# Gated slot attention: state matmuls ahead of the softmax transposes, and f and gate projections without a transpose

## The chip, the cores and the metric

The kernel runs on the 8 cores of one Trainium2 chip. Each core works on its own share of the batch, two sequences, with no exchange between cores. The metric is the device time of the slowest core in microseconds (us). Engines are TensorE (PE in the profile, its weight loads PEld), VectorE (DVE), ScalarE (ACT), GpSimd (POOL) and SyncE (SP). Each runs its own stream of instructions in order and waits for the others on semaphores.

## What is computed

One transformer layer on x of 16 x 2048 x 1024, float32. It has two halves with a residual each: gated slot attention, and a mixture of experts with top-1 routing. Cut to what matters, with H = 8 heads, DK = 128 and M = 64 slots:

```python
q, k, v = silu(x @ Wq), silu(x @ Wk), x @ Wv
log_f   = log_sigmoid(x @ Wf1 @ Wf2);  s = 1 - exp(log_f)
# per head, over time:
hk = hk * exp(log_f)[:, None] + k[:, None] * s[None, :];  ok = q @ hk
qv = softmax(ok)
hv = hv * exp(log_f)[:, None] + s[:, None] * v[None, :];  ov = qv @ hv
out = ov * sigmoid(x @ Wg1 @ Wg2);  out = rmsnorm_per_head(out) * norm_w
x = x + out @ Wo          # x on the right is the layer norm of the input
x = x + p_max * gelu(ln(x) @ W1[e]) @ W2[e]     # e = argmax of the router, 8 experts
```

## The kernel before

**Tiling.** A core does its two sequences b = 0, 1 one after the other: attention of b, then the FFN of b. The sequence lies in x_buf in SBUF. Attention goes through it in 16 segments of 128 positions, each of two chunks of 64. The recurrence is worked out per chunk, with the states a_hk and a_hv carried between them. The FFN then runs every expert over groups of 1024 positions. Its weights are converted to bf16 in DRAM by DMAs that start at the beginning.

**Order of the work.** The order is written out by hand: `P.op` (its issuing line is line 60 for all instructions of the profile) appends an instruction to the stream of an engine, `P.wait` a wait on a semaphore. On VectorE and ScalarE every operation waits for the one before it and increments a semaphore of its engine.

**Input groups.** `make_x_groups(s)` gives 17 groups for segment s: g1 (layer norm), g2 (transposes), six projections (q, k, v in halves, called q0, q1, k0, k1, v0, v1 here), g6 (the f gate: x @ Wf1, then @ Wf2), g6b and two g6c (the output gate), g7 (sigmoids), g8a and g8b (transposes of q and k), g9 and g9b (decay factors, with the triI and triL matmuls). Each group writes the one PSUM bank p_x; ScalarE evacuates it, and the next group waits for that (`px_wait`). The groups of segment 0 run ahead of the loop, as a prologue. For the others g1 goes ahead of `emit_y` of the segment before, and the rest are fed in by `inject()`, two groups at a call, of which `emit_y(s)` has two per chunk and two after both; g8a to g9b follow it. In the last segment of a sequence nothing is left to feed in.

**In g6 and g6b** the eight matmuls of x @ Wf1 (or Wg1) have the activations xnt as stationary operand and give a 128 x 128 result with positions as rows. It is evacuated (a_u, a_ug), transposed by TensorE, evacuated again (a_ut, a_ugt), and only then multiplied by Wf2 (Wg2).

**A chunk in `emit_y`**, in the order of TensorE's stream: the ones128 matmul into p_st (waiting for the state update and the output step before it), the 16 onescol matmuls into p_st with a small exp behind them (blast_act), 8 matmuls k.q into p_a, 16 into p_ok, `inject()`; VectorE and ScalarE work out the softmax of p_ok; 16 transposes into p_tp, 8 matmuls into p_a, 16 into p_ov; then 24 state matmuls: per head one of k and s into p_st and two of s and v into p_st2 (heads 0 to 3) or p_ok (heads 4 to 7); `inject()`. VectorE's state update (a_hk from p_st, then a_hv from p_st2 and p_ok, 8 operations) waits for the last of the 24. After both chunks: gate, norm, transposes into p_tp, 16 matmuls with Wo into p_ov, and the addition to x_buf.

Of the kernel before, what the change touches and what calls it, by code (L numbers as in the profile page):

```python
# [8 lines left out]
AF = mybir.ActivationFunctionType  # L9
# [70 lines left out]
def build_nc():  # L80
# [228 lines left out]
    def emit_attention(b):  # L309
# [17 lines left out]
        def px_wait():  # L327
            if "free" in px_state:
                P.wait(t, px_state["free"][0], px_state["free"][1])

        def make_x_groups(s):
# [49 lines left out]
            def g6():  # L381
                def small_mm_t(dst_sb, w1sb):
                    px_wait()
                    for dt in range(8):
                        p1 = P.op(t, "matmul", p_x[:, 0:DK],
                                  S["xnt"][:, dt * SEG:(dt + 1) * SEG],
                                  w1sb[:, dt * DK:(dt + 1) * DK],
                                  start=(dt == 0), stop=(dt == 7),
                                  inc="pe" if dt == 7 else None)
                    P.wait(a, "pe", p1)  # L390
                    e1 = P.op(a, "activation", dst_sb, p_x[:, 0:DK], AF.Copy,
                              inc="act")
                    evac_done("act")
                    return e1

                def tr(dst_sb, src_sb, e1):
                    px_wait()
                    p1 = P.op(t, "transpose", p_x_b[:, 0:DK], src_sb, id128[:],
                              inc="pe")
                    P.wait(a, "pe", p1)  # L400
                    e2 = P.op(a, "activation", dst_sb, p_x_b[:, 0:DK], AF.Copy,
                              inc="act")
                    evac_done("act")
                    return e2

                e1 = small_mm_t(a_u[:], a_wf1)
                e2 = tr(a_ut[:], a_u[:], e1)
# [8 lines left out]
            def g6b():  # L416
                def small_mm_t(dst_sb, w1sb):
                    px_wait()
                    for dt in range(8):
                        p1 = P.op(t, "matmul", p_x[:, 0:DK],  # L420
                                  S["xnt"][:, dt * SEG:(dt + 1) * SEG],
                                  w1sb[:, dt * DK:(dt + 1) * DK],
                                  start=(dt == 0), stop=(dt == 7),
                                  inc="pe" if dt == 7 else None)
# [584 lines left out]
```

How the kernel before makes its waits and increments, by code:

```python
        def f(e, fname=fname, args=args, kw=kw, h=h, amt=amt):  # L59
            ins = getattr(e, fname)(*args, **kw)
            if h is not None:
                ins.then_inc(h, amt)
# [8 lines left out]
        def f(e, h=h, val=val):  # L71
            e.wait_ge(h, val)
```

## Time and profile before

| | us |
|---|---|
| median of 2 timed runs | 12,627.6 |
| lowest, highest | 12,280.6, 12,974.7 |
| the profiled execution | 11,624.9 |
| its span, slowest core (core 3) | 11,623.4 |
| spans of the eight cores | 11,592.4 to 11,623.4 |
| mean granted TensorE clock of the cores | 0.843 to 0.845 |

The profile is of one execution, on its slowest core. The granted clock is a share of full speed: 1.00 is 2.4 GHz, 0.50 is 1.2 GHz. In a row of the timeline stand the start, the duration, the engine, the operation with what it writes and reads, how many instructions are merged, and in brackets how long the engine had been idle and what released it. The state matmuls show as p_st (64*128 64x64), and as p_st and p_ok (64*64 64x128); p_st2 is listed as p_st, and rows of the two forms are partly merged. Merged rows overlap a little, as the ends of matmuls are modelled.

### The profile page before, as it was taken

The numbers are of one execution on the slowest core, as the hardware profiler recorded it, in microseconds if no ns is written. First come the engines' busy times: TensorE is split into PE (matmuls) and PEld (weight loads), VectorE is DVE, ScalarE is ACT, GpSimd is POOL, SyncE is SP. The second block draws the span as 40 slices with busy tenths as digits, with TensorE's granted clock in tenths as the row PEclk, the third lists the DMA queues.
The fourth block names the chain that finished last, engine by engine and source line by source line (L and its number), as shares of the span: only waits on it lengthen the run. The fifth ranks groups of instructions, "written<-read, shape, count | busy, mean of one in ns | idle before, by whom it ended". The sixth has DMA issues, their size and how long they took to land.

```text
span 11623.4 us, 114796 instructions; the slowest of 8 cores (11592.4 to 11623.4 us)
## 1 busy us (share of the span) xinstructions
PE 9248.6 (80%) x44448; PEld 4228.6 (36%) x44448; DVE 1755.1 (15%) x2899; ACT 2237.4 (19%) x3340; POOL 1377.4 (12%) x2414
## 2 busy tenths in 40 slices
PE   2555555999999999999935555559999999999999
PEld 1222222444444444444412222224444444444443
DVE  2333333000000000000023333330000000000000
ACT  1212222211121112211112122222112211122111
POOL 0000000111111111111100000001111111111111
PEclk7555556999999999999955555579999999999999
DMA  9999501333333433333330000013333334333333
GB/s 139 110 110 109 58 1 33 93 110 111 104 98 104 124 116 96 105 102 109 108 73 1 1 1 1 1 33 100 108 115 98 102 104 122 112 98 102 107 109 114
DMA packets 262991, 999.45 MB, mean 86 GB/s; under 512 B 44832, under 2 KB 45088, under 8 KB 258352
## 3 DMA queue, kind: packets, MB, share of 16 engines
q0 software_dynamic: 254176, 958.56, 34.7%
q1 hardware_dynamic: 8288, 33.55, 0.8%
q8 instruction: 369, 6.05, 0.2%
q14 instruction: 158, 1.29, 0.0%
HBM read 1128.14 MB, written 150.99 MB: 110 GB/s over the span
## 4 chain that ended last, share of the span: by engine, by line
PE 76%; DVE 11%; ACT 6%; issue 4%; another core or an unknown queue 2%; DMA 1%; DVEq 0%; ACTq 0%; POOL 0%; POOLq 0%
PE p_ov L60 26%; PE p_st L60 24%; PE p_x L60 9%; DVE arena L60 8%; PE p_ok L60 6%; ACT arena L60 5%; PE p_tp L60 5%; PE p_a L60 4%; DVE x_buf L60 3%; ACT L60 1%; DMA arena<-w2sc 1%; DVEq L72 0%; ACTq L72 0%; DMA arena<-wr 0%
## 5 line engine op out<-in xcount | busy, mean ns | idle before, releaser
L60 PE MATMUL p_ov<-arena 128*128 128x512 bf16 (+1 forms) x13824 | 3484.9, 389 | 338.5 <-DVE x_buf L60 170.9
L60 PE MATMUL p_st<-arena 128*128 128x512 bf16 (+2 forms) x13312 | 3267.7, 373 | 20.4 <-DVE x_buf L60 20.4
L60 PEld LDWEIGHTS p_ov<-arena 128*128 128x128 bf16 (+1 forms) x13824 | 1392.2, 106 | 2008.6 <-issue 634.5
L60 PEld LDWEIGHTS p_st<-arena 128*128 128x128 bf16 (+2 forms) x13312 | 1291.3, 99 | 1578.7 <-issue 80.8
L60 PE MATMUL p_x<-arena 128*128 128x512 bf16 (+2 forms) x4448 | 1511.7, 427 | 221.7 <-ACT arena L60 213.1
L60 ACT ACTIVATE arena<-p_ov,arena 128x512 bf16<-128x512 f32 x1024 | 703.6, 687 | 4672.2 <-PE p_ov L60 4624.5
L60 POOL DMA_DIRECT2D arena<-w2sc x2048 | 1099.5, 537 | 3474.6 <-PE p_tp L60 3473.0
L60 DVE SCALAR_TENSOR_TENSOR x_buf<-p_ov,arena,x_buf 128x512 f32<-128x512 f32 x128 | 96.1, 750 | 7028.1 <-PE p_tp L60 7021.1
L60 PE MATMUL p_ok<-arena 128*128 128x512 bf16 (+3 forms) x3584 | 1062.5, 337 | 73.7 <-DVE arena L60 64.7
L60 PE MATMUL p_a<-arena 128*128 128x512 bf16 (+2 forms) x3072 | 862.5, 333 | 90.5 <-DVE arena L60 81.5
L60 ACT ACTIVATE arena<-p_st,arena 128x512 bf16<-128x512 f32 x1024 | 703.7, 687 | 1040.6 <-PE p_st L60 991.2
L60 PE MATMUL p_tp<-arena 128*128 128x512 bf16 x2048 | 785.7, 384 | 8.6 <-DVE x_buf L60 8.6
L60 PEld LDWEIGHTS p_x<-arena 128*128 128x128 bf16 x4448 | 448.1, 113 | 883.4 <-issue 605.9
L60 ACT ACTIVATE arena<-p_x 128x512 bf16<-128x512 f32 (+3 forms) x512 | 305.9, 597 | 2098.7 <-PE p_x L60 2093.0
L60 POOL DMA_DIRECT2D arena<-w1sc x256 | 226.9, 888 | 3124.7 <-PE p_st L60 2695.8
L60 PE MATMUL p_tp<-id,arena 64*64 64x64 bf16 (+2 forms) x1600 | 130.0, 253 | 562.2 <-DVE arena L60 544.1
L60 PE MATMUL p_x<-id,arena 128*128 128x128 bf16 x832 | 109.8, 294 | 528.4 <-DVE arena L60 369.0
L60 PEld LDWEIGHTS p_ok<-arena 128*128 128x128 bf16 (+2 forms) x3584 | 362.4, 110 | 414.0 <-issue 104.5
L60 DVE TENSOR_TENSOR arena<-arena 64x512 f32<-64x512 f32 (+5 forms) x484 | 349.1, 721 | 940.0 <-ACT arena L60 542.8
L60 POOL DMA_DIRECT2D arena<-b x4 | 2.1, 523 | 3582.3 <-DVE x_buf L60 3582.3
L60 PEld LDWEIGHTS p_a<-arena 128*128 128x128 bf16 (+2 forms) x3072 | 261.1, 113 | 357.2 <-issue 122.8
L60 PEld LDWEIGHTS p_tp<-id,arena 64*64 64x64 bf16 (+2 forms) x1600 | 108.0, 142 | 631.8 <-issue 631.8
(84 smaller groups left out, 2536.5 us busy)
## 6 DMA issues: line engine op xcount, KB each, us to landing
arena<-w2sc POOLq DMA_DIRECT2D x2048, 256.0 KB, 2.9
arena<-w1sc POOLq DMA_DIRECT2D x256, 1024.0 KB, 6.1
w1sc<-w POOLq DMA_DIRECT2D x8, 8192.0 KB, 418.2
w2sc<-w POOLq DMA_DIRECT2D x8, 8192.0 KB, 1027.0
x_buf<-x SPq DMA_DIRECT2D x2, 8192.0 KB, 44.7
y<-x_buf SPq DMA_DIRECT2D x4, 4096.0 KB, 12.2
arena<-wq POOLq DMA_DIRECT2D x2, 2048.0 KB, 30.5
arena<-wk POOLq DMA_DIRECT2D x2, 2048.0 KB, 45.9
```

What stands on the lines that cost most here:

```text
L60: ins = getattr(e, fname)(*args, **kw)
```

## The change

In g6 and g6b the operands of the eight matmuls are swapped, so that the result comes out transposed, and the transpose and one evacuation are dropped. In each chunk, the eight p_st state matmuls are issued behind the first `inject()`, and the sixteen p_st2 and p_ok ones behind them with a wait for the VectorE product that reads p_ok; both groups stand ahead of the wait for the softmax. The state update waits for the last p_ov matmul. The number of state matmuls and their operands are the same.

```diff
--- before.py
+++ after.py
@@ -379,32 +379,17 @@
                 return f
 
             def g6():
-                def small_mm_t(dst_sb, w1sb):
-                    px_wait()
-                    for dt in range(8):
-                        p1 = P.op(t, "matmul", p_x[:, 0:DK],
-                                  S["xnt"][:, dt * SEG:(dt + 1) * SEG],
-                                  w1sb[:, dt * DK:(dt + 1) * DK],
-                                  start=(dt == 0), stop=(dt == 7),
-                                  inc="pe" if dt == 7 else None)
-                    P.wait(a, "pe", p1)
-                    e1 = P.op(a, "activation", dst_sb, p_x[:, 0:DK], AF.Copy,
-                              inc="act")
-                    evac_done("act")
-                    return e1
-
-                def tr(dst_sb, src_sb, e1):
-                    px_wait()
-                    p1 = P.op(t, "transpose", p_x_b[:, 0:DK], src_sb, id128[:],
-                              inc="pe")
-                    P.wait(a, "pe", p1)
-                    e2 = P.op(a, "activation", dst_sb, p_x_b[:, 0:DK], AF.Copy,
-                              inc="act")
-                    evac_done("act")
-                    return e2
-
-                e1 = small_mm_t(a_u[:], a_wf1)
-                e2 = tr(a_ut[:], a_u[:], e1)
+                px_wait()
+                for dt in range(8):
+                    p1 = P.op(t, "matmul", p_x[:, 0:SEG],
+                              a_wf1[:, dt * DK:(dt + 1) * DK],
+                              S["xnt"][:, dt * SEG:(dt + 1) * SEG],
+                              start=(dt == 0), stop=(dt == 7),
+                              inc="pe" if dt == 7 else None)
+                P.wait(a, "pe", p1)
+                e2 = P.op(a, "activation", a_ut[:], p_x[:, 0:SEG], AF.Copy,
+                          inc="act")
+                evac_done("act")
                 px_wait()
                 P.wait(t, "act", e2)
                 p1 = P.op(t, "matmul", p_x[:], a_ut[:], a_wf2[:], start=True,
@@ -414,25 +399,15 @@
                 evac_done("act")
 
             def g6b():
-                def small_mm_t(dst_sb, w1sb):
-                    px_wait()
-                    for dt in range(8):
-                        p1 = P.op(t, "matmul", p_x[:, 0:DK],
-                                  S["xnt"][:, dt * SEG:(dt + 1) * SEG],
-                                  w1sb[:, dt * DK:(dt + 1) * DK],
-                                  start=(dt == 0), stop=(dt == 7),
-                                  inc="pe" if dt == 7 else None)
-                    P.wait(a, "pe", p1)
-                    e1 = P.op(a, "activation", dst_sb, p_x[:, 0:DK], AF.Copy,
-                              inc="act")
-                    evac_done("act")
-                    return e1
-                e3 = small_mm_t(a_ug[:], a_wg1)
                 px_wait()
-                p1 = P.op(t, "transpose", p_x_b[:, 0:DK], a_ug[:], id128[:],
-                          inc="pe")
+                for dt in range(8):
+                    p1 = P.op(t, "matmul", p_x[:, 0:SEG],
+                              a_wg1[:, dt * DK:(dt + 1) * DK],
+                              S["xnt"][:, dt * SEG:(dt + 1) * SEG],
+                              start=(dt == 0), stop=(dt == 7),
+                              inc="pe" if dt == 7 else None)
                 P.wait(a, "pe", p1)
-                xs["ugt"] = P.op(a, "activation", a_ugt[:], p_x_b[:, 0:DK], AF.Copy,
+                xs["ugt"] = P.op(a, "activation", a_ugt[:], p_x[:, 0:SEG], AF.Copy,
                                  inc="act")
                 evac_done("act")
 
@@ -582,12 +557,20 @@
                                tile_position=(0, pi * 64),
                                inc="pe" if h == 7 else None)
                 inject()
+                P.wait(t, "act", ys["blast_act"])
+                for h in range(H):
+                    P.op(t, "matmul", p_st[:, h * 64:h * 64 + 64],
+                         S["ktm"][rs, h * 128:(h + 1) * 128],
+                         S["stb"][rs, h * 64:(h + 1) * 64],
+                         start=True, stop=True, tile_position=(pi * 64, 0),
+                         inc="pe" if h == 7 else None)
                 P.wait(v, "pe", pok)
                 okb = a_otmp[rs, 0:512]
                 qvt = a_otmp[rs, 512:1024]
                 okb3 = okb.rearrange("p (h m) -> p h m", m=64)
                 qvt3 = qvt.rearrange("p (h m) -> p h m", m=64)
-                P.op(v, "tensor_tensor", okb, p_ok[rs, :], S["B"][rs, :], ALU.mult)
+                okb_dve = P.op(v, "tensor_tensor", okb, p_ok[rs, :], S["B"][rs, :],
+                               ALU.mult, inc="dve")
                 P.op(v, "tensor_reduce", a_nmx[rs, :], okb3, axis=AX.X, op=ALU.max,
                      negate=True)
                 sm_dve = P.op(v, "tensor_tensor", qvt3, okb3,
@@ -602,6 +585,18 @@
                      a_rsum[rs, :].unsqueeze(2).broadcast_to([64, 8, 64]), ALU.mult)
                 qb_dve = P.op(v, "tensor_tensor", a_qb[rs, :], qvt, S["B"][rs, :],
                               ALU.mult, inc="dve")
+                P.wait(t, "dve", okb_dve)
+                for h in range(H):
+                    sbc = S["stb"][rs, h * 64:(h + 1) * 64]
+                    vv = S["vtm"][rs, h * 128:(h + 1) * 128]
+                    bank2 = p_st2 if h < 4 else p_ok
+                    for base in (0, 64):
+                        pov_st = P.op(t, "matmul",
+                                      bank2[base:base + 64,
+                                            (h % 4) * 128:(h % 4 + 1) * 128],
+                                      sbc, vv, start=True, stop=True,
+                                      tile_position=(pi * 64, base),
+                                      inc="pe" if (h == 7 and base == 64) else None)
                 P.wait(t, "dve", qb_dve)
                 for h in range(H):
                     oc = h * 64
@@ -635,25 +630,14 @@
                     P.op(t, "matmul", p_ov[rs, h * 128:(h + 1) * 128],
                          a_atm[rs, h * 64:h * 64 + 64], vv,
                          start=True, stop=False, tile_position=(pi * 64, pi * 64))
-                    P.op(t, "matmul", p_ov[rs, h * 128:(h + 1) * 128],
-                         a_qbt[rs, oc:oc + 64], a_hv[rs, h * 128:(h + 1) * 128],
-                         start=False, stop=True, tile_position=(pi * 64, pi * 64))
-                for h in range(H):
-                    sbc = S["stb"][rs, h * 64:(h + 1) * 64]
-                    vv = S["vtm"][rs, h * 128:(h + 1) * 128]
-                    P.op(t, "matmul", p_st[:, h * 64:h * 64 + 64],
-                         S["ktm"][rs, h * 128:(h + 1) * 128],
-                         sbc, start=True, stop=True, tile_position=(pi * 64, 0))
-                    bank2 = p_st2 if h < 4 else p_ok
-                    for base in (0, 64):
-                        pov = P.op(t, "matmul",
-                                   bank2[base:base + 64,
-                                         (h % 4) * 128:(h % 4 + 1) * 128],
-                                   sbc, vv, start=True, stop=True,
-                                   tile_position=(pi * 64, base),
-                                   inc="pe" if (h == 7 and base == 64) else None)
+                    ov_pe = P.op(t, "matmul", p_ov[rs, h * 128:(h + 1) * 128],
+                                 a_qbt[rs, oc:oc + 64],
+                                 a_hv[rs, h * 128:(h + 1) * 128],
+                                 start=False, stop=True,
+                                 tile_position=(pi * 64, pi * 64),
+                                 inc="pe" if h == 7 else None)
                 inject()
-                P.wait(v, "pe", pov)
+                P.wait(v, "pe", ov_pe)
                 P.wait(v, "act", bca_act)
                 P.op(v, "tensor_tensor", a_hkt, a_hk, a_bca, ALU.mult)
                 P.op(v, "tensor_tensor", a_hk, a_hkt, p_st[:], ALU.add)
```

## Rows read from the trace of the kernel before

**Rows 1.** The page: busy TensorE and its granted clock in 40 slices, tenths.
```profile
PE   2555555999999999999935555559999999999999
...
PEclk7555556999999999999955555579999999999999
```

**Rows 2.** Busy time by stretch: PE, PEld, DVE, ACT, POOL, then granted clock, DMA.
```profile
100.00:1860.00 1760.00, 897.12 (x5352) 461.88 (x5352) 615.75 (x1104) 370.41 (x586) 3.73 (x5) 0.59 0.70 77
...
2300.00:5800.00 3500.00, 3364.37 (x15120) 1486.99 (x15118) 174.06 (x232) 619.79 (x902) 619.36 (x1082) 0.97 0.36 107
```

**Rows 3.** Timeline, first chunk: start, duration, engine, operation, idle before and its releaser.
```profile
1018.83 3.08 PE L60 MATMUL p_ok<-arena 64*64 64x64 bf16 x16 [1.01 <-DVE arena L60]
...
1022.08 0.68 DVE L60 TENSOR_TENSOR arena<-p_ok,arena 64x512 f32<-64x512 f32 x1 [3.40 <-PE p_ok L60]
...
1024.19 3.40 PE L60 MATMUL p_x<-arena 128*128 128x512 bf16 x8 [1.32 <-ACT arena L60]
...
1028.44 0.63 ACT L60 ACTIVATE arena<-arena 64x512 f32<-64x512 f32 x1
...
1031.93 1.03 PE L60 MATMUL p_tp<-id,arena 64*64 64x64 bf16 x16 [4.34 <-DVE arena L60]
...
1035.94 1.88 PE L60 MATMUL p_ov<-arena 64*64 64x128 bf16 x16 [1.12 <-DVE arena L60]
...
1037.75 1.86 PE L60 MATMUL p_st<-arena 64*128 64x64 bf16 x13
...
1041.02 3.54 PE L60 MATMUL p_x<-arena 128*128 128x512 bf16 x8
...
1041.34 0.43 DVE L60 TENSOR_TENSOR arena<-arena 128x512 bf16<-128x512 bf16 x1 [5.66 <-PE p_ok L60]
...
1044.46 1.70 DVE L60 SCALAR_TENSOR_TENSOR arena<-arena,p_ok 128x128 bf16<-128x128 bf16 x4
...
1045.45 1.89 PE L60 MATMUL p_x<-arena 128*128 128x512 bf16 x8 [0.89 <-ACT arena L60]
...
1047.27 0.39 PE L60 MATMUL p_st<-arena,ones 64*128 64x512 bf16 x1
```

**Rows 4.** Timeline, second chunk and the head of what follows it.
```profile
1064.41 0.74 PE L60 MATMUL p_tp<-id,arena 64*64 64x64 bf16 x16 [4.36 <-DVE arena L60]
...
1070.13 1.87 PE L60 MATMUL p_st<-arena 64*128 64x64 bf16 x13
...
1073.72 0.43 DVE L60 TENSOR_TENSOR arena<-arena 128x512 bf16<-128x512 bf16 x1 [5.82 <-PE p_ok L60]
...
1086.98 1.01 PE L60 MATMUL p_tp<-id,arena 128*128 128x128 bf16 x8 [1.32 <-DVE arena L60]
```

**Rows 5.** Timeline of TensorE in the prologue of the first batch.
```profile
135.50 0.22 PE L60 MATMUL p_x<-id,arena 128*128 128x128 bf16 x1 [0.57 <-ACT arena L60]
...
136.40 0.58 PE L60 MATMUL p_x<-arena 128*128 128x512 bf16 x1 [0.68 <-ACT arena L60]
```

**Rows 6.** Timeline: triI matmul of g9 for segments 1, 2, 3 and 15 (of 0 to 15).
```profile
263.86 0.64 PE L60 MATMUL p_x<-arena,triI 64*64 64x512 bf16 x2 [4.42 <-DVE arena L60]
...
367.26 0.64 PE L60 MATMUL p_x<-arena,triI 64*64 64x512 bf16 x2 [4.42 <-DVE arena L60]
...
475.76 0.64 PE L60 MATMUL p_x<-arena,triI 64*64 64x512 bf16 x2 [4.43 <-DVE arena L60]
...
1742.99 0.64 PE L60 MATMUL p_x<-arena,triI 64*64 64x512 bf16 x2 [4.43 <-DVE arena L60]
```

**Rows 7.** Granted clock around q1 of rows 3; a slow q1 and k0, second segment.
```profile
1038.00:1041.00 3.00, 3.00 (x23) 1.65 (x23) 0.00 (x0) 0.00 (x0) 0.00 (x0) 0.50 1.18 131
...
1044.00:1045.00 1.00, 0.56 (x2) 0.00 (x0) 0.78 (x3) 0.29 (x1) 0.00 (x0) 0.81 0.31 33
...
403.88 3.60 PE L60 MATMUL p_x<-arena 128*128 128x512 bf16 x8
...
408.37 3.57 PE L60 MATMUL p_x<-arena 128*128 128x512 bf16 x8 [0.89 <-ACT arena L60]
```

## The prediction

> **What bounds the kernel now.** I read the strip of forty slices first, then the busy times by stage, then the timeline of one segment, then the starts of all segments.
>
> The strip shows four stages: two stretches in which TensorE is about half busy at about half of its full clock (slices 2 to 7 and 22 to 27), each followed by a long stretch at 9 and near full clock [rows 1]. The busy times by stage put numbers on it. In the first attention stretch (100 to 1860 us) TensorE works 897 of 1760 us, VectorE 616 and ScalarE 370, at a mean granted clock of 0.59; the second looks the same in the strip. In the FFN stretch TensorE works 3364 of 3500 us at 0.97 [rows 2]. So the FFN is bound by TensorE, and attention by no engine: it is a chain of short steps in which the engines wait for each other. The diff touches only attention. Whatever it saves there starts the FFN earlier by the same time; the FFN itself should not change.
>
> The timeline of one segment shows where the chain runs. A segment has two chunks. In the first one TensorE ends projection q0 at 1027.59 (1024.19 + 3.40), and then sits idle for 4.34 us until the softmax chain on ScalarE (exp at 1028.44, queued behind the evacuation of q0) and VectorE frees the 16 transposes at 1031.93. Then come p_ov at 1035.94 and, right behind it, the 24 state matmuls, from 1037.75 to the start of the next projection q1 at 1041.02. VectorE starts the state update only after them, at 1041.34 [rows 3]. The second chunk repeats it: idle until the transposes at 1064.41, state matmuls at 1070.13, state update at 1073.72 [rows 4].
>
> **The change, part by part.**
>
> 1. *The 24 state matmuls move* from behind p_ov to a place between the first pair of injected projections and the softmax transposes. What they leave: from 1037.75 to 1041.02 they take 3.27 us of TensorE. In the first chunk q1 stood right behind them, and behind q1 come its evacuation, k0 (1045.45) and, at 1047.27, the matmul that opens the next chunk. That matmul also waits for the state update. The update's last group starts at 1044.46 and takes 1.70, so it ends at 1046.16, 1.1 us before the opener [rows 3]. Both branches start 3.27 us earlier, so the opener does too. In the second chunk VectorE's chain (state update at 1073.72, then gate, norm and scale up to the transposes at 1086.98, 13.26 us later) sets the end. It begins 3.59 us after the state matmuls begin (1070.13), just as in the first chunk (1037.75 to 1041.34) [rows 3, 4]. With the wait on p_ov alone it begins 3.27 us earlier. So 2 x 3.27 = 6.54 us leave each segment.
>
> 2. *Where they go.* The eight p_st matmuls need only the small exp, long done; the other sixteen need the VectorE product that reads p_ok, which starts at 1022.08 and takes 0.68, done 4.8 us before q0 ends [rows 3]. So all 24 can start at 1027.59 without a wait. The place has 4.34 us. The price is at most what they cost in the old order, 3.27 us or 0.136 each, and at least 2.8 us if all went at the p_ov price (1.88 / 16 = 0.117 each). Even the interleaved p_ok group (3.08 / 16 = 0.193 each, the dearest narrow row) would make 4.6 us, 0.3 over the gap [rows 3]. In the new order the two forms stand in separate groups, so I take something at or below 3.27 and nothing on the path. If the p_ok price held, it would cost 0.3 x 64 = 19 us. ScalarE has both projection evacuations and exp in its queue ahead of anything the moved matmuls could delay. The new wait for the VectorE product has only the sixteen matmuls and the transposes behind it, and is released earlier.
>
>    In the last segment of a batch nothing is injected. There the moved matmuls meet the wait for the p_ok product, but have the whole softmax chain as cover, from 1022.08 to 1031.93 less the evacuation of q0. All 2 x 16 segments save the same: 32 x 6.54 = 209 us.
>
> 3. *f and gate projections without the transposes.* The eight matmuls swap operands and yield the transposed result directly; a transpose, its wait and its evacuation leave. In the prologue this is on the chain: from the transpose at 135.50 to the next matmul at 136.40 is 0.90 us [rows 5]. Two such places in each of two batches give 3.6 us. Within segments the same work lies beside VectorE's 13.26 us chain of the second chunk [rows 4]: nothing. If that cover were gone, it would be worth 0.9 x 2 x 30 = 54 us more.
>
> 4. *Waits.* The VectorE product's added semaphore costs nothing, since every VectorE operation increments one already.
>
> Sum: 209 + 3.6 = 213 us. The profiled execution took 11,624.9 us (span 11,623.4), so its own time would become 11,412. The two timed runs of the kernel lie at 12,280.6 and 12,974.7, median 12,627.6: well above the profiled one, and 694 us apart. Carried over to the median: 12,627.6 - 213 = 12,415.
>
> **The clock.** The level that TensorE is granted moves the segment time. The first interval between segments is 103.40 us, the second 108.50, and the mean of the fourteen between 263.86 and 1742.99 is 105.65 [rows 6]. The difference is the projections: k0 takes 1.89 us at the upper level (2.4 GHz) and 3.57 at the lower (1.2 GHz) [rows 3, 7]. What raises the level? While p_ov and the state matmuls kept TensorE fully busy the granted clock stayed at 0.50; it rose only when q1, which starts at 1041.02, was ending (0.81 over 1044 to 1045) [rows 7]. No rise followed directly on the stretch that is taken away, and q1 and k0 themselves stay as they are. So I take the mix of fast and slow segments to stay too.
>
> Against that stands a rule. The Trainium skill, in "TensorE: Matmul & The Clock Gate", section "Why this matters for your kernels", advises keeping TensorE continuously busy to get past its throttled state. By the rule, taking 3.27 us of unbroken work away ahead of q1 would lose fast groups. The rows just named speak against it, and another pair does: q1 and k0 of the second segment stood behind the same unbroken state matmuls, and k0 was slow all the same [rows 7].
>
> **The rivals.**
>
> - *Clock lost.* If every segment after were like the slowest (108.50 instead of 105.65), the loss is 2.85 x 30 = 86 us, and 127 us remain: 12,501. For it: the removed unbroken stretch. Against it: the rows above. 10%.
> - *Clock gained.* If every one were like the fastest (103.40), 2.25 x 30 = 68 us more, 281 us in all: 12,347. For it: a shorter segment packs its projections closer. Against: nothing makes the projections themselves denser. 14%.
> - *Half of it.* One chunk's saving is taken by another wait, for instance because in the first chunk the update proves late and the opener waits for VectorE. The margin is 1.1 us here, and both sides move together. 105 + 3.6 = 109 us: 12,519. 6%.
> - *Slower.* The FFN runs at another granted clock. It is the only stage large enough: two FFN stretches, the first with 3364 of 3500 us of TensorE work [rows 2] and the second alike in the strip. A granted clock lower by 3% in both costs 0.03 x 2 x 3364 = 202 us and eats the saving; to end over 2% slower it takes 213 + 253 = 466 us, a clock lower by 7%. For it: the 694 us between two runs of one kernel, which no latency-bound stage could give. Against: nothing in the change touches the FFN. A draw of that kind may fall either way. I give it 30%: 20% that it makes the result more than 2% faster, 4% within, 6% slower.
> - The forecast as it stands: 40%.
>
> **How the numbers follow.** Two per cent of 12,628 is 253 us, about what a measurement of this kernel can tell from no change. The forecast (213, 1.7%) lies inside, clock lost and half inside too, clock gained outside. Faster: 14 + 20 = 34%; within: 40 + 10 + 6 + 4 = 60%; slower: 6%. The likeliest case alone, with runs like the median, saves 194 (the p_ok price) to 213 us, 12,415 to 12,434. The full range must hold the spread of the runs: from the profiled execution less 213, 11,410, to the slower run less 213, 12,760.
>
> **What would show it.** Right: the 24 matmuls stand at the end of q0, end before the transposes, and the idle time ahead of the transposes shrinks from 4.34 us to 1.1 us or a little more, the transposes not later; VectorE's update starts 0.2 to 0.3 us after p_ov ends; segment starts are 99 us apart on average instead of 105.65; the FFN stretches are as long as before. Wrong: transposes later than 4.34 us behind q0 (cover too small), a mean segment above 101 us with k0 and v0 mostly at 3.57 us (clock), the opener waiting for VectorE (half).

## The result and the profile after

| | kernel before | changed kernel |
|---|---|---|
| median of the timed runs, us | 12,338.6 (10 runs) | 12,152.3 (11 runs) |
| lowest run, us | 11,623.2 | 11,398.1 |
| profiled execution, us | 11,624.9 | 11,398.3 |
| first attention stretch, us | 1715.7 | 1600.1 |
| second attention stretch, us | 1710.9 | 1603.0 |
| first FFN stretch to the next batch, us | 4089.8 | 4089.0 |

The changed kernel is faster: the ratio of like runs is 0.9807, with a 95% interval from 0.9779 to 0.9836. Whether the gain is more or less than 2% this leaves open. An attention stretch is counted from TensorE's first instruction of a batch to the 32 small transposes that open the FFN (113.67 to 1829.41 and 5919.16 to 7630.10 before, 104.59 to 1704.71 and 5793.72 to 7396.71 after). The runs of one kernel differ by several hundred us, because in many of them the cores of a die get a lower clock in the FFN; so attention stretches are compared below.

The strip of the page after, busy TensorE and its granted clock in tenths, keeps the shape of [rows 1], with attention stretches that end earlier:

```profile
PE   3445546999999999999834545469999999999998
...
PEclk7565558999999999999955565589999999999999
```

Busy time by stretch after (columns as in [rows 2]). Attention is still far from full on any engine, at a granted clock of 0.60 (0.59 before), and the FFN still has 0.97:

```profile
100.00:1700.00 1600.00, 788.88 (x5187) 425.60 (x5264) 588.50 (x1069) 356.81 (x545) 0.55 (x2) 0.60 0.76 83
...
2300.00:5500.00 3200.00, 3054.80 (x13570) 1361.26 (x13845) 162.12 (x216) 594.96 (x866) 551.02 (x956) 0.97 0.37 106
```

The timeline of two chunks after answers to [rows 3, 4]. The trace has lost one matmul record of some projection groups, which is why they read "x7" and seem to start 0.4 us late. (p_st2 is again listed as p_st.)

```profile
1050.11 0.68 DVE L60 TENSOR_TENSOR arena<-p_ok,arena 64x512 f32<-64x512 f32 x1 [3.40 <-PE p_ok L60]
...
1052.60 3.19 PE L60 MATMUL p_x<-arena 128*128 128x512 bf16 x7 [1.70 <-DVE arena L60]
...
1055.72 1.17 PE L60 MATMUL p_st<-arena 64*128 64x64 bf16 x16
...
1056.68 0.64 PE L60 MATMUL p_ok<-arena 64*64 64x128 bf16 x8
...
1060.13 1.03 PE L60 MATMUL p_tp<-id,arena 64*64 64x64 bf16 x16 [2.81 <-DVE arena L60]
...
1064.14 1.88 PE L60 MATMUL p_ov<-arena 64*64 64x128 bf16 x16 [1.12 <-DVE arena L60]
...
1066.27 0.42 DVE L60 TENSOR_TENSOR arena<-arena 128x512 bf16<-128x512 bf16 x1 [2.39 <-PE p_ov L60]
...
1066.36 3.19 PE L60 MATMUL p_x<-arena 128*128 128x512 bf16 x7 [0.33 <-issue]
...
1069.39 1.70 DVE L60 SCALAR_TENSOR_TENSOR arena<-arena,p_ok 128x128 bf16<-128x128 bf16 x4
...
1070.44 3.57 PE L60 MATMUL p_x<-arena 128*128 128x512 bf16 x8 [0.89 <-ACT arena L60]
...
1073.95 0.60 PE L60 MATMUL p_st<-arena,ones 64*128 64x512 bf16 x1
...
1088.30 0.74 PE L60 MATMUL p_st<-arena 64*128 64x64 bf16 x16
...
1088.88 0.39 PE L60 MATMUL p_ok<-arena 64*64 64x128 bf16 x8
...
1092.72 1.03 PE L60 MATMUL p_tp<-id,arena 64*64 64x64 bf16 x16 [3.45 <-DVE arena L60]
...
1098.89 0.42 DVE L60 TENSOR_TENSOR arena<-arena 128x512 bf16<-128x512 bf16 x1 [2.38 <-PE p_ov L60]
```

The 16 matmuls of p_st and p_st2 stand at the end of q0 (1055.72), the 8 of p_ok behind them. All 24 are through at 1057.32, after 1.60 us at the lower clock; in the second chunk, at the upper one, from 1088.30 they take 0.97 us. TensorE then still waits 2.81 us for the softmax. p_ov ends at 1066.02, and VectorE's update starts 0.25 us later, at 1066.27. It ends at 1071.09, 2.9 us ahead of the opener of the next chunk at 1073.95. So TensorE's q1 and k0 set the end of the first chunk, as they did before (the margin was 1.1 us there; k0 is slow here and was fast there).

The 226.6 us between the two profiled executions add up so. TensorE's first instruction comes 9.1 us earlier (104.59 in place of 113.67); over the eight cores of all these kernels it lies anywhere from 102 to 116 us, so that is no effect of the change. Attention gives 115.6 and 107.9 us. The first FFN stretch is 0.7 us shorter, and the rest of the run, from the second FFN start to the end, is 6.7 us longer. These are two single cores. In means over the eight cores an attention stretch takes 1712.6 us before and 1598.5 after, 114.1 less.

### The profile page after: what moved, and what is told of

Same layout as the page of the kernel before. It is cut to its first block, busy times and chain, and to the rows that moved or that the text cites. A ratio compares the mean times of both kernels' runs of the same rounds, so it can differ in the third digit from the quotient of the medians.

```text
span 11396.7 us, 113717 instructions; the slowest of 8 cores (11362.1 to 11396.7 us)
## 1 busy us (share of the span) xinstructions
PE 8997.2 (79%) x43561; PEld 4163.8 (37%) x44384; DVE 1755.5 (15%) x2899; ACT 2219.0 (19%) x3276; POOL 1377.2 (12%) x2414
## 4 chain that ended last, share of the span: by engine, by line
PE 74%; DVE 12%; ACT 6%; issue 4%; another core or an unknown queue 2%; DMA 1%; DVEq 1%; ACTq 0%; POOL 0%; POOLq 0%
PE p_ov L60 27%; PE p_st L60 23%; DVE arena L60 9%; PE p_x L60 9%; PE p_ok L60 6%; ACT arena L60 5%; PE p_tp L60 5%; PE p_a L60 4%; DVE x_buf L60 3%; ACT L60 1%; DMA arena<-w2sc 1%; DVEq L72 1%; ACTq L72 0%; DMA arena<-wr 0%
## 5 line engine op out<-in xcount | busy, mean ns | idle before, releaser
L60 PE MATMUL p_ov<-arena 128*128 128x512 bf16 (+1 forms) x13556 | 3438.4, 388 | 361.3 <-DVE x_buf L60 179.6
L60 PE MATMUL p_st<-arena 128*128 128x512 bf16 (+2 forms) x13054 | 3132.7, 370 | 40.5 <-DVE x_buf L60 23.6
L60 PEld LDWEIGHTS p_st<-arena 128*128 128x128 bf16 (+1 forms) x13312 | 1248.5, 99 | 1546.8 <-issue 114.8
L60 PE MATMUL p_x<-arena 128*128 128x512 bf16 (+2 forms) x4221 | 1423.8, 423 | 306.2 <-ACT arena L60 216.5
L60 PE MATMUL p_ok<-arena 128*128 128x512 bf16 (+3 forms) x3584 | 1012.8, 328 | 77.4 <-DVE arena L60 64.7
L60 PE MATMUL p_a<-arena 128*128 128x512 bf16 (+2 forms) x3002 | 837.3, 333 | 90.5 <-DVE arena L60 81.5
L60 ACT ACTIVATE arena<-p_x 128x512 bf16<-128x512 f32 (+1 forms) x448 | 287.9, 643 | 1888.4 <-PE p_x L60 1599.6
```

Source lines behind the costliest of these rows:

```text
L60: ins = getattr(e, fname)(*args, **kw)
```

## The experiments

The table has one core of each kernel, for the doubled kernel ("moved, twice") two. Over the eight cores of a profile a first or second stretch varies by 2 to 18 us in most kernels. It varies by 50 and 36 us in the doubled kernel, and by 40 us in the first stretch of the last one. "Fast" counts the projection groups (eight 128x512 matmuls) that took 1.89 us, of 192; the prologues hold up to ten of them.

| kernel | core | attention stretches, us | mean segment interval in each, us | fast |
|---|---|---|---|---|
| before | 3 | 1715.7, 1710.9 | 105.8, 105.8 | 42 |
| changed | 0 | 1600.1, 1603.0 | 98.8, 99.0 | 41 |
| only moved | 4 | 1601.9, 1602.5 | 99.0, 98.9 | 43 |
| only projections | 3 | 1709.8, 1712.4 | 105.8, 105.8 | 38 |
| only regrouped, old place | 0 | 1656.9, 1655.7 | 102.4, 102.4 | |
| moved, not regrouped | 4 | 1595.2, 1602.6 | 98.6, 99.0 | |
| moved, twice | 0 | 1655.1, 1643.7 | 102.2, 101.5 | 24 |
| the same profile | 3 | 1606.5, 1615.2 | 99.0, 99.8 | 65 |
| first chunk only | 0 | 1645.2, 1654.3 | 101.6, 102.2 | |
| second chunk only | 0 | 1659.5, 1655.9 | 102.5, 102.4 | |
| changed, 1 copy more | 0 | 1601.0, 1607.2 | 99.0, 99.2 | 66 |
| changed, 3 copies more | 4 | 1655.4, 1654.9 | 102.4, 102.5 | 40 |
| changed, fillers | 4 | 1597.9, 1593.3 | 98.9, 98.4 | 41 |
| changed, p_ok grouped | 4 | 1547.9, 1544.7 | 95.6, 95.4 | 39 |
| the same, again | 5 | 1545.3, 1542.2 | 95.6, 95.2 | |
| p_ok grouped and fillers | 4 | 1515.4, 1547.6 | 93.6, 95.6 | |

The count varies from core to core too: 37 to 43 in the kernel before, 40 to 47 in the changed one. Two of the three runs of the kernel "first chunk only" took 22,377 and 24,624 us, and one of nine of "the same, again" 25,992 us; why isn't on record.

**Which half of the diff gains.** First the move alone, with the projections of the kernel before:

```diff
-                for dt in range(8):
-                    p1 = P.op(t, "matmul", p_x[:, 0:SEG], a_wf1[...], S["xnt"][...], ...)
+                e1 = small_mm_t(a_u[:], a_wf1)
+                e2 = tr(a_ut[:], a_u[:], e1)
```

> The changed kernel with the f and gate projections of the kernel before (transposes kept), so only the state matmuls are moved. Theory (the moved matmuls carry the gain): about 223 us under the kernel before in like runs (11,400 to 11,405), mean segment interval 99.0 us, as in the changed kernel. Rival (the dropped transposes count within segments): at least 50 us less gain, 11,450 or more.

The stretches are 1601.9 and 1602.5 us, the changed kernel's to 2 us, and the mean interval is 99.0 us, as expected. Then the projections alone, in the kernel before:

```diff
-                e1 = small_mm_t(a_u[:], a_wf1)
-                e2 = tr(a_ut[:], a_u[:], e1)
+                for dt in range(8):
+                    p1 = P.op(t, "matmul", p_x[:, 0:SEG], a_wf1[...], S["xnt"][...], ...)
```

> The kernel before with only the f and gate projections changed (operands swapped, no transposes). Theory: covered by VectorE's chain within segments, 3.6 us in the prologues, about 11,621 in a like run, mean segment interval unchanged at 105.7 us. Rival (half hidden): 30 us or more less and an interval 1 us shorter.

1709.8 and 1712.4 us against 1715.7 and 1710.9. The interval stays at 105.8, and 30 us are excluded: the transposes in the groups were hidden. The effect forecast for the prologues, 1.8 us each, is lost in the spread of single stretches, but not in the prologues themselves. From TensorE's first instruction of a batch to the first triI matmul they take 43.6 us before and 42.0 with the projections alone, in means over eight cores and both batches (44.3 with the move alone, 41.8 in the changed kernel). The move is the gain.

**Each chunk by itself.** The move is made where `c4` is 0, or where it is 1; in the other chunk the 24 stay behind p_ov.

```diff
+                if c4 == 0:      # second kernel: c4 == 1
+                    P.wait(t, "dve", okb_dve)
+                    for h in range(H):
+                        ...
+                if c4 != 0:
+                    for h in range(H):
+                        ... as in the kernel before, behind p_ov
```

> State matmuls moved (grouped) in the first chunk of each segment only; the second chunk and the f and gate projections as in the kernel before. Theory (each chunk gives its own 3.27 us, here by way of TensorE's order): mean segment interval 105.8 - 3.3 = 102.5 us, attention stretch 1713 - 54 = 1659. Rival (only the second chunk's move pays, as there VectorE's chain is the longer): 105.8 and 1713.

> State matmuls moved in the second chunk only; the first chunk and the projections as in the kernel before. Theory: here VectorE's chain starts 3.27 us earlier, mean interval 102.5 us, stretch 1659. Rival (the first chunk carries it all): 105.8 and 1713.

Each gives about half: 1645 to 1654 us and 1656 to 1660 us. Both chunks lay on the way to the end, as forecast. That it was TensorE's order in the one and VectorE's chain in the other is read from the rows, and neither run separates them.

**Is it the place or the grouping?** The diff does two things to the state matmuls: it moves them, and it issues eight of one tile form and then sixteen of another in place of alternating per head. Grouping alone, in the old place:

```diff
                 for h in range(H):
-                    sbc = ...; vv = ...
-                    P.op(t, "matmul", p_st[:, h * 64:h * 64 + 64], ...)
+                    P.op(t, "matmul", p_st[:, h * 64:h * 64 + 64], ...)
+                for h in range(H):
+                    sbc = ...; vv = ...
                     bank2 = p_st2 if h < 4 else p_ok
                     for base in (0, 64):
```

> The kernel before with the 24 state matmuls left behind p_ov, but issued as eight p_st ones and then sixteen p_st2/p_ok ones instead of alternating per head. Theory 1 (alternating between tile forms is what cost 3.27 us; grouped the 24 take 1.60 us as in the changed kernel at the lower clock): 1.67 us less per chunk, 64 x 1.67 = 107 us, about 11,518, and VectorE's state update starts 1.9 us after p_ov ends. Theory 2 (they were short in the changed kernel because of their place, behind an idle stretch or at another clock): no gain, 11,625.

Timeline on core 5, behind p_ov (TensorE, then VectorE's update):

```profile
1028.15 1.88 PE L60 MATMUL p_ov<-arena 64*64 64x128 bf16 x16 [1.28 <-DVE arena L60]
...
1029.96 1.17 PE L60 MATMUL p_st<-arena 64*128 64x64 bf16 x16
...
1030.92 0.63 PE L60 MATMUL p_ok<-arena 64*64 64x128 bf16 x8
...
1031.49 3.19 PE L60 MATMUL p_x<-arena 128*128 128x512 bf16 x8
...
1031.81 0.42 DVE L60 TENSOR_TENSOR arena<-arena 128x512 bf16<-128x512 bf16 x1 [4.08 <-PE p_ok L60]
```

From 1029.96 to the next projection at 1031.49 the 24 take 1.53 us in place of 3.27, and the update starts 1.78 us after p_ov ends. The stretches fall by 59 and 55 us, to 1656.9 and 1655.7: half of the gain of the change is to be had without moving anything. So alternating was dear. Then the other way round, the new place with the old order:

```diff
-                for h in range(H):
-                    P.op(t, "matmul", p_st[...], ..., tile_position=(pi * 64, 0), ...)
-                P.wait(t, "dve", okb_dve)   # behind the softmax product's issue
+                P.wait(t, "dve", okb_dve)
+                for h in range(H):
+                    P.op(t, "matmul", p_st[...], ..., tile_position=(pi * 64, 0))
+                    ... the two of bank2
```

> The changed kernel with the state matmuls in the new place, but alternating per head as in the kernel before. Theory (the cover of 4.34 us holds either order): the 24 take 3.27 us, the idle time of TensorE ahead of the softmax transposes is 1.1 us in place of 2.8, and the time equals the changed kernel's within 10 us (11,400). Rival (the grouping matters for the time): about 100 us slower than the changed kernel, 11,500.

1595.2 and 1602.6 us: the changed kernel's time. Alternating is dear here too: TensorE's idle time ahead of the transposes is 1.45 us in first chunks and 1.91 in second ones, in means over eight cores, where the changed kernel has 3.10 and 3.46. But the order doesn't matter for the time, because the gap covers either. That the gap is a cover of limited size shows when the alternating 24 are issued twice each (extra work):

```diff
-                for h in range(H):
+                for h in [hh for hh in range(H) for _ in range(2)]:
```

> The changed kernel with the state matmuls alternating per head and each issued twice, in the new place: 48 matmuls, 6.54 us by the rows of the kernel before, in a gap of 4.34 us. Theory (the gap is a cover of that size): the softmax transposes come 2.2 us late in each chunk, mean segment interval 98.9 + 4.4 = 103.3 us, stretch about 1670. Rival (the gap is not what limits): 1600 us as before, or the whole 3.27 us a chunk on top, 1705.

Timeline, TensorE, second chunk of a segment on core 1:

```profile
1018.60 2.26 PE L60 MATMUL p_x<-arena 128*128 128x512 bf16 x8 [0.89 <-ACT arena L60]
...
1020.79 2.76 PE L60 MATMUL p_st<-arena 64*128 64x64 bf16 x25
...
1025.84 0.31 PE L60 MATMUL p_ok<-arena 64*64 64x128 bf16 x2
...
1025.96 1.05 PE L60 MATMUL p_tp<-id,arena 64*64 64x64 bf16 x16
```

v0 ends at 1020.86, the 48 fill the time to the transposes at 1025.96, and no idle time stands ahead of these. They come 5.1 us behind v0 in place of 4.36, here with part of the group at the upper clock. In means of the eight cores they come 5.4 to 6.2 us behind q0 and 5.0 to 5.2 behind v0 (4.4 in both places in the changed kernel), with no idle time ahead of them in any segment. So the gap is a cover of limited size, and what sticks out is 1.6 to 2.6 us a segment, where 4.4 was expected at the lower clock throughout.

What becomes of that differs within the same profile. On core 0 the stretches are 55 and 41 us longer than in the changed kernel. On core 3 they are 6 and 12 us longer, and the first stretches of cores 6 and 7 are 1605.2 and 1606.9 us, with the changed kernel's interval of 99.0. The rival of no effect nearly holds there, and the whole 6.5 us a segment is found nowhere. A segment of core 3 (q0, the transposes, k0, v0):

```profile
1062.47 3.23 PE L60 MATMUL p_x<-arena 128*128 128x512 bf16 x8 [1.32 <-ACT arena L60]
...
1070.99 1.06 PE L60 MATMUL p_tp<-id,arena 64*64 64x64 bf16 x16
...
1080.62 1.89 PE L60 MATMUL p_x<-arena 128*128 128x512 bf16 x8 [0.89 <-ACT arena L60]
...
1093.48 1.89 PE L60 MATMUL p_x<-arena 128*128 128x512 bf16 x8 [0.89 <-ACT arena L60]
```

There k0 was fast in all 30 segments and v0 in 27, on core 0 in 17 and 4. Faster groups took back most of what the late transposes cost. The next two experiments show the same.

**Why 6.9 us a segment where 6.54 were taken away.** A known delay is put on the path: the copy of a_qbt on VectorE is made once more, or three times more.

```diff
                 P.op(v, "tensor_copy", a_qbt[rs, :], p_tp[rs, 0:512])
+                P.op(v, "tensor_copy", a_qbt[rs, :], p_tp[rs, 0:512])
```

> The changed kernel with one redundant copy more on VectorE in each chunk, on the path between the softmax transposes and p_a (the copy of a_qbt made twice; a copy starts every 0.52 us). Adding up rows: 2 x 0.52 = 1.0 us a segment, mean interval 99.9, stretch 1617. If the mix of fast and slow projection groups shifts against it, as it may have done in the change (6.9 us gained where 6.54 were taken away): the interval stays at 98.9 to 99.2, stretch 1600 to 1604.

> The same with three redundant copies more in each chunk, 6 x 0.52 = 3.1 us a segment. Adding up rows: mean interval 102.0, stretch 1650. If the mix shifts: back to the 102.4 us that the kernel with regrouped matmuls in the old place had, stretch 1656, with fewer fast groups than the 41 of 187 of the changed kernel.

Starts of the triI matmul in the second batch, segments 0 and 15, in the kernel before, the changed one, and with one and three copies more:

```profile
5961.71 0.63 PE L60 MATMUL p_x<-arena,triI 64*64 64x512 bf16 x2 [4.43 <-DVE arena L60]
...
7549.29 0.64 PE L60 MATMUL p_x<-arena,triI 64*64 64x512 bf16 x2 [4.43 <-DVE arena L60]
```

```profile
5837.40 0.64 PE L60 MATMUL p_x<-arena,triI 64*64 64x512 bf16 x2 [4.43 <-DVE arena L60]
...
7321.92 0.64 PE L60 MATMUL p_x<-arena,triI 64*64 64x512 bf16 x2 [4.43 <-DVE arena L60]
```

```profile
5826.86 0.64 PE L60 MATMUL p_x<-arena,triI 64*64 64x512 bf16 x2 [4.43 <-DVE arena L60]
...
7315.14 0.64 PE L60 MATMUL p_x<-arena,triI 64*64 64x512 bf16 x2 [4.43 <-DVE arena L60]
```

```profile
5901.75 0.64 PE L60 MATMUL p_x<-arena,triI 64*64 64x512 bf16 x2 [4.43 <-DVE arena L60]
...
7438.50 0.63 PE L60 MATMUL p_x<-arena,triI 64*64 64x512 bf16 x2 [4.43 <-DVE arena L60]
```

A fifteenth of each difference is the mean interval: 105.84, 98.97, 99.22 and 102.45 us. One copy more adds 1.04 us of work to a segment and 0.25 us to the interval. Three add 3.12 us and the interval grows by 3.5. The mix of fast and slow groups answers. Within segments only k0 and v0, the second of their pairs, were ever at 1.89 us. Of their 60 groups 32 were fast in the kernel before, 58 with one copy more and 30 with three. In means, k0 and v0 took 2.84 and 2.49 us before, 2.90 and 2.34 in the only moved kernel, 1.95 and 1.95 with one copy more, 2.06 and 3.40 with three. Wo (the 16 matmuls into p_ov at the segment's end) goes the other way with one copy more, 6.3 us where the changed kernel has 5.5, and takes 5.6 with three.

The intervals found in the kernels without fillers lie near 105.8, 102.4, 98.9 and 95.5 us, each 3.4 to 3.5 us from the next, whatever was added or taken. The first-chunk kernel (101.6 in one of its stretches) and the doubled one (99.8 to 102.2 besides 99.0) come off these. In means over eight cores and both batches:

| change | taken from or added to a segment, us | interval, us |
|---|---|---|
| grouping in the old place | -3.5 | 105.82 to 102.35 |
| the move alone | -6.5 | 105.82 to 98.86 |
| the changed kernel | -6.5 | 105.82 to 98.75 |
| one copy more in it | +1.0 | 98.75 to 99.08 |
| three copies more in it | +3.1 | 98.75 to 102.42 |
| p_ok grouped in it (below) | -3.8 | 98.75 to 95.43 |

So a change moves the mean interval by about 0, one or two steps of 3.4 us, whichever is nearest. That the interval moves in steps is shown; why the steps are of this size no run shows.

**Can the clock be raised?** Idle time of TensorE is filled with full-width matmuls whose result nobody reads, in three gaps of each chunk.

```diff
+                for _ in range(5):
+                    P.op(t, "matmul", p_a[:], a_wq[:, 0:128], a_wq[:, 0:512],
+                         start=True, stop=True)
                 P.wait(t, "dve", qb_dve)
... (two into p_a ahead of tt_dve's wait, two into p_x ahead of atm2_dve's)
```

> The changed kernel with idle time of TensorE filled by full-width matmuls whose result nobody reads (extra work, the output is unaffected): five ahead of the softmax transposes, two between the transposes and p_a, two between p_a and p_ov, in each chunk. Theory (the clock level is what makes a segment long or short, and TensorE's wide work raises it): more of the projection groups take 1.89 us instead of 3.57 than the 41 of 187 of the changed kernel, and the attention stretch falls below 1600 us, by up to 90 (about 6 us a segment if all of them were fast, 1510). Rival (the gaps don't matter to the level, or the fillers run over the gaps): 1600 us or more.

Timeline, first chunk of a segment, slowest core (core 7):

```profile
1067.87 1.25 PE L60 MATMUL p_a<-arena 128*128 128x512 bf16 x5
...
1071.38 0.66 PE L60 MATMUL p_tp<-id,arena 64*64 64x64 bf16 x16 [2.26 <-DVE arena L60]
...
1071.97 0.60 PE L60 MATMUL p_a<-arena 128*128 128x512 bf16 x2
...
1073.71 1.03 PE L60 MATMUL p_x<-arena 128*128 128x512 bf16 x2
...
1074.89 1.88 PE L60 MATMUL p_ov<-arena 64*64 64x128 bf16 x16
...
1076.71 3.60 PE L60 MATMUL p_x<-arena 128*128 128x512 bf16 x8
```

The five fillers ahead of the transposes and the two behind them ran at the upper clock (0.25 to 0.30 us each). The last two (1.03 us) were back at the lower one, and the eight matmuls of q1, behind p_ov, still took 3.60 us. 41 of 192 groups were fast, as before (36 to 44 over the eight cores). Stretches of 1597.9 and 1593.3 us are 2 to 10 us better; in means over the cores it is 1 us. The theory failed in this form.

**The same cost elsewhere.** The 16 matmuls of p_ok alternate two forms as well (3.08 us in [rows 3]) and stand on the path. They are grouped; the start flag is set at head 0 alone.

```diff
+                for h in range(H):
+                    P.op(t, "matmul", p_ok[rs, oc], a_atm[rs, oc], S["stl"][...],
+                         start=(h == 0), stop=False, tile_position=(pi * 64, pi * 64))
                 for h in range(H):
-                    P.op(t, "matmul", p_ok[rs, oc], a_atm[rs, oc], ..., start=True, ...)
-                    pok = P.op(..., S["qt"][:, tc], a_hk[:, oc], start=False, stop=True, ...)
+                    pok = P.op(..., S["qt"][:, tc], a_hk[:, oc], start=False, stop=(h == 7), ...)
```

> The changed kernel with the 16 p_ok matmuls grouped as well: first the eight of 64 rows (a_atm), then the eight of 128 rows, instead of alternating per head. Theory (alternating forms is what is dear, and this group stands on the path in both chunks): the group takes 1.2 to 1.3 us (eight p_a matmuls of either form take 0.60 to 0.64) instead of 3.08, so about 1.85 us less per chunk, 64 x 1.85 = 118 us, an attention stretch of about 1541 us in place of 1600, about 11,280 in a run like the profiled one. Rival (the alternation costs nothing, K = 128 or the accumulation does): no gain.

Timeline, the p_ok group in both chunks of a segment and the transposes that follow the first:

```profile
1024.69 1.17 PE L60 MATMUL p_ok<-arena 64*64 64x64 bf16 x16 [1.00 <-DVE arena L60]
...
1025.79 1.03 PE L60 MATMUL p_x<-id,arena 128*128 128x128 bf16 x8
...
1053.21 1.03 PE L60 MATMUL p_ok<-arena 64*64 64x64 bf16 x16 [1.01 <-DVE arena L60]
```

1.17 us in place of 3.08, both at the lower clock, and stretches of 1547.9 and 1544.7 us, 52 and 58 less than in the changed kernel. The grouping also parts the two matmuls that add to the same sum. That this was dear is unlikely: the p_ov matmuls of [rows 3] add up in such pairs, in one form, and take 0.117 us each with twice the columns, where p_ok alternating took 0.193. It was run again:

> The kernel with the grouped p_ok matmuls once more, timed in more rounds beside the kernel before. Theory: the attention stretch is again 1540 to 1548 us, the mean interval 95.2 to 95.6, and the fastest run lies 112 + 227 = 339 us under the fastest of the kernel before, near 11,285. Rival (the shorter attention is paid back by a longer FFN): the first FFN stretch is longer than 4093 us and the fastest run no better than the changed kernel's 11,398.

The stretches repeat (1545.3 and 1542.2; 1542.8 and 1541.6 on core 7), and the first FFN stretch is 4087 us, no longer than before. Its fastest run took 11,299.3 us (11,285 was expected), beside 11,625.1 for the fastest of the kernel before: 326 us, 2.8%, and 99 us under the changed kernel's fastest. This kernel beats both. With the fillers added:

> The grouped p_ok matmuls and the fillers together (the fillers are extra work whose result nobody reads). If both theories hold and add: attention stretch about 1450 to 1540 us, 11,100 to 11,280. If the shorter p_ok group leaves less work ahead of q0 and the clock falls back: no better than the grouped one alone.

1515.4 and 1547.6 us, and a fastest run of 11,275.3 us, 24 us less. The first stretch is 32 us shorter and the second 3 us longer than with the grouping alone. The other cores agree: the first stretch is 1513 to 1531 us on six of eight (1546 to 1553 on cores 2 and 3), against 1545 to 1552 with the grouping alone, and the second one doesn't gain on any. So the fillers gained something in one place, with an interval of 93.3 to 94.6 us that no other kernel has; why not in the other stretch stays open. Of a single pair of fastest runs 24 us would prove nothing.

## Why the prediction was right and wrong

**The mechanism was right.** Moved matmuls leave the path and are covered, in both chunks, VectorE's update starts 0.25 us after p_ov, the FFN is untouched. In attention the two stretches gave 223.6 us on the cores read, and 228 in means over the eight cores, against 213 forecast.

**The term that was mis-sized is 6.54 us a segment.** It was 6.9 on the cores read (105.84 to 98.97), and 7.07 in means over eight cores and both batches (105.82 to 98.75). The 228 us add up so: 30 intervals of 7.07 make 212 where 196 were forecast, the two last segments about 6.3 each (6.54 forecast), and the two prologues 1.7 each (1.8). So the intervals alone are off. The step that failed is "So I take the mix of fast and slow segments to stay too": the interval does not follow the sum of what is on the path, it moves in steps of about 3.4 us, and 6.54 us taken away became two of them. How the two came to differ is found in the durations in part. In these means v0 takes 2.50 us before and 2.34 after, Wo 5.63 and 5.47, k0 2.83 and 2.85: 0.3 of the 0.5 us. The number of fast groups hardly changed. The rest is open. The doubled kernel and the copies show that the answer of the mix can be larger than the difference here, 1 us a segment and more.

**What was wrong is the step from the sum to the chances.** I gave 60% to "within 2%", on the ground that 2% is "about what a measurement of this kernel can tell", and 30% to a draw of the FFN's clock. The comparison of like runs tells 0.3%. The gain of 1.9% is a clear one, and a sum of 213 us against runs of 11,625 us (1.8%) should have been called a small but sure gain. The 694 us between the first two runs misled me. Those two left no clocks on record, but in the later profiles such differences lie in the FFN's clock, and they don't enter such a comparison. This clock is seen in one profile of the doubled kernel: busy time and granted clock over 2300 to 5500 us on core 7 and on core 1, of the other die.

```profile
2300.00:5500.00 3200.00, 3080.59 (x13307) 1337.03 (x13306) 150.13 (x200) 571.65 (x832) 531.24 (x923) 0.93 0.34 102
```

```profile
2300.00:5500.00 3200.00, 3073.78 (x13837) 1361.21 (x13836) 162.15 (x216) 571.59 (x832) 565.54 (x987) 0.97 0.36 107
```

The span is 12,370.6 us on core 7 and 11,502.6 on core 1, with 1606.9 and 1651.9 us in the first attention stretch: core 7 is slower for its FFN, not for attention. So the rival "slower" named the right stage for the spread, and was wrong to give it a share of the verdict. (Its price was low too: 3364 us are the work of a window of 3500, and the first FFN stretch lasts 4089.8.) The time itself, 12,152 us at the median, lies in the range; the 12,415 was carried over from a median of two runs that ten runs put at 12,338.6. From that median 213 us would have led to 12,126, and what remains lies within the spread of the runs: that a median comes so close is luck. Like for like, 11,412 was forecast and 11,398.3 measured.

**The cover.** The 24 were priced at 2.8 to 3.27 us and took 1.60 and 0.97. The floor was taken from p_ov, whose 16 matmuls sit on one tile position (0.117 us each); grouped, the sixteen that alternate between two column halves and the eight of p_st take 0.067 us each. It cost nothing here, as the gap held all of it, but it hid the other half of the finding: grouping without moving gives 55 to 59 us a stretch.

**Clock lost** did not come. The fast groups number 42 before and 41 after on the cores read, 41 and 43 in means over eight. The Trainium skill's advice in "TensorE: Matmul & The Clock Gate", section "Why this matters for your kernels", to keep TensorE busy without a break, would have k0 slower after the move. The traces don't agree: k0 takes 2.83 us before (mean of eight cores) and 2.83 with the move alone (mean of cores 4 to 7). **Half of it** came only where half the change was made. **The projections** were hidden in the segments, as forecast; of their 3.6 us in the prologues 3.1 to 3.5 were found against the kernel before.

## What to carry to other kernels

In a stage in which engines wait for each other in a chain, look for work that only the end of the step needs and put it where its engine idles; check the size of the gap. Then look at small matmuls that alternate tile forms: order them by form first, since here it was worth half as much as the move and needed no gap, and a second such group was worth as much again. Where the fast and slow groups of a loop can change places, a known saving may come back larger or smaller: 1.04 us added to each segment cost 0.25, and 3.12 cost 3.5. So measure the loop's mean interval on all cores and in several variants before a difference of a microsecond is explained by a sum.

## What the runs showed of the hardware

- **Alternating tile forms is dear.** Eight matmuls of 64 rows by 128 columns and sixteen of 64 by 64 took 3.27 us alternating and 1.53 to 1.60 grouped, at the lower clock. Sixteen of p_ok, 64 and 128 rows deep, took 3.08 us alternating and 1.17 grouped. The Trainium skill states the cause in "TensorEngine Tiling (Array Packing)", section "Key Properties": a change of tiling mode, not of tile, drains TensorE. The traces agree that the change costs: both regroupings leave 14 changes of form fewer, and 3.27 - 1.60 = 1.67 and 3.08 - 1.17 = 1.91 us make 0.12 and 0.14 us a change. That it is a drain no row shows.
- **Segment intervals settle at a few values**, 105.8, 102.4, 98.9 and 95.5 us: 1.04 us of work added to every segment changed the mean interval by 0.25 us, with 66 fast projection groups in place of 41, and 3.12 us changed it by 3.5. In the doubled kernel one profile holds stretches at 99.0 and at 102.2 us for the same program.
- **The spread between runs is the FFN's.** The clock over 2300 to 5500 us fell from 0.97 to 0.93 on the core above. In the kernel with three copies the first FFN stretch took 4670.5 us on core 7 and 4092.9 on core 4, and the two attention stretches 1658.4 and 1658.1 against 1655.4 and 1654.9. In two kernels the cores with the slow first FFN had a longer first attention stretch too: 1661.0 us on core 4 against 1645.2 on core 0 (first chunk only), and 1552.9 on core 2 against 1515.4 on core 4 (p_ok grouped and fillers).
